# Self-attention block, 16 images, 8 heads: scores of a head made once in blocks of 128 queries instead of a maximum pass over 512 queries and a second score pass

## The chip, the cores and the metric

The kernel runs on one core of one Trainium2 chip. A core has four engines that compute, each with its own instruction stream: TensorE (matmuls, called PE in the profile; its weight loads are PEld), VectorE (DVE), ScalarE (ACT) and GpSimd (POOL). SyncE (SP) issues the DMA transfers. Engines meet only at semaphores. TensorE writes to PSUM, eight banks of 512 f32 columns on 128 partitions; VectorE and ScalarE read it, GpSimd cannot. The metric is the device time of the program in microseconds (us); lower is better.

## The reference

```python
B, N, heads, d = 16, 32 * 32, 8, 64            # 512 channels
qkv  = x @ w_qkv + b_qkv                        # [B, N, 8, 192]
q, k, v = split(qkv, 3)
attn = softmax(einsum('bxhd,byhd->bxyh', q, k) * d ** -0.5, over y)
res  = einsum('bxyh,byhd->bxhd', attn, v)
out  = res @ w_out + b_out + x
```

Input, weights and output are f32.

## The kernel before

**Precision.** Every operand is split into a high f16 part and a low f16 part (the rest), and a product is made of three f16 matmuls, hi x hi, hi x lo and lo x hi, summed in f32 in PSUM.

**Staging.** For each of the 16 images the kernel projects q and k of one head for 512 tokens at a time (12 matmuls of 512 columns, `fill`, L577), v for 128 tokens and four heads at a time (12 of 256 columns), runs attention per head, transposes the result (`transpose`, L586) and projects it (12 of 512 columns). Splitting is done by ScalarE (high parts) and VectorE (low parts).

**Attention.** Scores are kept transposed, keys on partitions and queries on columns, so that the exponentials are at once the stationary operand of the value product. The softmax then needs its maximum as a term of the product: rows of `k_shift` hold the constant 4096 and rows of `q_shift` hold minus the maximum over 4096, so the second matmul of each score tile (L634) adds both the low part of q and the shift. A unit is 512 queries of one head; its work is:
- first pass (`row_max_tile`, L596): q stationary, 512 keys on columns, 8 matmuls; VectorE reduces each to a maximum per query (L852). The results are joined (L856), transposed (L604) and written as shift rows (L862).
- second pass (`step_scores`, L632 and L634): for each of 8 key tiles two matmuls of 512 columns.
- two exponentials of each tile (`exp_tile`): f32 (`p_full`, L747) and f16 (`p_hi`, L748). Their difference is `p_lo`, made by GpSimd in six of eight steps (L493) and by VectorE in two (L871). A step is two key tiles, 1024 columns.
- values (`step_pv`, L657 to L662): per key tile and 128 queries hi x v_hi with a column of ones that gives the sum, hi x v_lo, lo x v_hi, mostly 65 columns wide. The division (L884 to L893) follows each unit.

**Order.** Tables of slots (a slot is a step) say at which slot each projection, transpose, maximum or split is issued; each engine walks the same slots and does its share, and a semaphore count per kind of work joins them. PSUM: score tiles rotate over three banks, so a tile's first matmul waits for the exponential three tiles back (L630); maxima and shift rows share two banks, fills two, and values one. In a slot TensorE issues maxima, one score tile of the next step, fills, the other score tile, late maxima, and the values of the step before:

```python
L630  wait(pe, exp_done, KEYS_PER_STEP * g + n + 1 - len(SCORE_BANKS))
```

## Time and profile before

| | |
|---|---|
| median of 3 runs | 3604.11 us (3601.85 to 3605.69) |
| profiled execution | 3603.24 us |
| its span | 3600.7 us |
| busy: TensorE, ScalarE, VectorE, GpSimd | 98%, 84%, 75%, 54% |
| mean granted TensorE clock | 0.999 of full speed |
| DMA | 144.70 MB, mean 40 GB/s |

The span reaches from the first to the last instruction in the trace. Busy time counts an instruction from its start to its end. Matmuls overlap: one is issued before the one ahead of it has ended, so what a matmul costs TensorE is the gap from its start to the next start, and that is read from the timeline. The chain that ended last is followed back from the last instruction to what released it or to the instruction before it on its engine.

### The profile page before, as it was taken

What the parts mean: (1) busy time and instruction counts of PE and PEld (TensorE: products, weight loads), DVE (VectorE), ACT (ScalarE), POOL (GpSimd) and SP (SyncE); (2) the same over time, 40 slices, a digit from 0 to 9 for tenths busy, and PEclk for the clock granted to TensorE, in tenths of its full rate; (3) what the DMA queues carried; (4) which work ended last, traced back from release to release, by engine and by line L of the source; (5) the groups of instructions that cost most, each with busy time, mean ns of one, the idle gap of its engine ahead of it and who ended that gap; (6) DMA issues with size and microseconds to landing.
All of it is one profiled execution on the core that took longest, in us unless ns stands there. A gap on an engine that the chain in (4) does not pass through costs nothing.

```text
span 3600.7 us, 93452 instructions
## 1 busy us (share of the span) xinstructions
PE 3527.6 (98%) x37132; PEld 2155.3 (60%) x37132; DVE 2689.1 (75%) x4643; ACT 3015.9 (84%) x5142; POOL 1949.6 (54%) x1022
## 2 busy tenths in 40 slices
PE   7999999999999999999999999999999999999998
PEld 4656566665666656666665666656666566665664
DVE  6777777777777777777777777777777777777775
ACT  6888878888788887888878788787888878888786
POOL 2564654556455564565645556455565555656545
PEclk9999999999999999999999999999999999999999
DMA  2011110111102011020110101112011110111101
GB/s 91 12 47 40 47 43 16 54 34 50 42 15 62 28 50 42 14 68 21 49 42 26 60 18 48 43 30 60 16 47 42 43 46 18 47 43 37 45 16 54
DMA packets 100709, 144.70 MB, mean 40 GB/s; under 512 B 16192, under 2 KB 48960, under 8 KB 100288
## 3 DMA queue, kind: packets, MB, share of 16 engines
q1 hardware_dynamic: 100288, 138.74, 13.0%
q8 instruction: 307, 5.03, 0.6%
q14 instruction: 114, 0.93, 0.1%
HBM read 71.57 MB, written 33.55 MB: 29 GB/s over the span
## 4 chain that ended last, share of the span: by engine, by line
PE 84%; ACT 5%; POOL 4%; issue 3%; DVE 2%; DMA 0%; SPq 0%; ACTq 0%; DVEq 0%
PE psum L577 33%; PE psum L596 11%; PE psum L632 10%; PE psum L634 10%; PE psum L659 4%; PE psum L657 4%; PE psum L658 4%; POOL p_lo L493 3%; PE psum L662 3%; ACT p_full L747 2%; ACT p_hi L748 2%; PE psum L586 2%; PE psum L661 1%; POOL xT_lo L487 1%; PE psum L604 1%
## 5 line engine op out<-in xcount | busy, mean ns | idle before, releaser
L493 POOL TENSOR_TENSOR p_lo<-p_full,p_hi 128x1024 f16<-128x1024 f32 x768 | 1635.5, 2130 | 1511.7 <-ACT p_hi L748 1511.7
L852 DVE TENSOR_REDUCE max_parts<-psum 128x1 f32<-128x512 f32 x2048 | 1369.1, 683 | 427.0 <-PE psum L596 425.7
L747 ACT ACTIVATE p_full<-psum,prob_bias 128x512 f32<-128x512 f32 x2048 | 1430.5, 698 | 176.8 <-PE psum L634 152.3
L748 ACT ACTIVATE p_hi<-psum,prob_bias 128x512 f16<-128x512 f32 x2048 | 1431.5, 699 | 0.0
L632 PE MATMUL psum<-q_hi_hi,k_lo_hi 128*128 128x512 f16 x2048 | 777.1, 379 | 18.2 <-ACT p_hi L748 10.3
L634 PE MATMUL psum<-q_shift,k_shift 128*128 128x512 f16 x2048 | 776.2, 379 | 0.0
L657 PE MATMUL psum<-v_parts,p_hi 128*128 128x65 f16 x6144 | 754.3, 192 | 12.0 <-POOL p_lo L493 12.0
L596 PE MATMUL psum<-k_lo_hi,q_hi_hi 128*128 128x512 f16 x2048 | 743.9, 380 | 16.8 <-DMA q_hi_hi<-q_hi_hi 4.7
L658 PE MATMUL psum<-v_parts,p_hi 128*128 128x64 f16 x6144 | 755.1, 193 | 0.0
L659 PE MATMUL psum<-v_parts,p_lo 128*128 128x65 f16 x6144 | 753.0, 194 | 0.0
L657 PEld LDWEIGHTS psum<-v_parts,p_hi 128*128 128x128 f16 x6144 | 585.8, 98 | 136.1 <-issue 22.8
L658 PEld LDWEIGHTS psum<-v_parts,p_hi 128*128 128x128 f16 x6144 | 573.3, 97 | 112.4
L659 PEld LDWEIGHTS psum<-v_parts,p_lo 128*128 128x128 f16 x6144 | 574.9, 97 | 0.0
L662 PE MATMUL psum<-v_parts,p_hi 128*128 128x129 f16 x2048 | 448.1, 219 | 0.0
L862 DVE SCALAR_TENSOR_TENSOR q_shift<-psum,identity 4x512 f16<-4x512 f32 x256 | 173.7, 679 | 315.2 <-PE psum L604 311.2
L577 PE MATMUL psum<-xT_hi,wqkv_hi 128*128 128x512 f16 x1024 | 388.8, 380 | 15.0 <-DVE xT_lo L805 15.0
L661 PE MATMUL psum<-v_parts,p_lo 128*128 128x65 f16 x2048 | 393.7, 192 | 0.0
L577 PE MATMUL psum<-xT_lo,wqkv_hi 128*128 128x512 f16 x1024 | 388.6, 380 | 0.0
L577 PE MATMUL psum<-xT_hi,wqkv_lo 128*128 128x512 f16 x1024 | 388.6, 380 | 0.0
L871 DVE TENSOR_TENSOR p_lo<-p_full,p_hi 128x1024 f16<-128x1024 f32 x256 | 318.2, 1243 | 37.5 <-ACT p_hi L748 33.5
L634 PEld LDWEIGHTS psum<-q_shift,k_shift 128*128 128x128 f16 x2048 | 200.3, 98 | 199.8
L596 PEld LDWEIGHTS psum<-k_lo_hi,q_hi_hi 128*128 128x128 f16 x2048 | 198.2, 97 | 186.3 <-DVE max_parts L852 76.5
(72 smaller groups left out, 4894.7 us busy)
## 6 DMA issues: line engine op xcount, KB each, us to landing
y_tile<-in_x SPq DMA_DIRECT2D x125, 256.0 KB, 2.8
result<-y_tile SPq DMA_DIRECT2D x125, 256.0 KB, 2.0
x_in<-in_xT SPq DMA_DIRECT2D x121, 256.0 KB, 2.9
q_hi_hi<-q_hi_hi SPq DMA_DIRECT2D x256, 64.0 KB, 1.9
k_shift<-k_lo_hi SPq DMA_DIRECT2D x256, 64.0 KB, 1.9
o_heads<-in_L_conv_w_qkv SPq DMA_DIRECT2D x12, 256.0 KB, 4.7
p_full<-in_xT SPq DMA_DIRECT2D x4, 256.0 KB, 5.2
o_heads<-in_L_conv_w_out SPq DMA_DIRECT2D x4, 256.0 KB, 3.0
```

What stands on the lines that cost most here:

```text
L493: nc.gpsimd.tensor_tensor(p_lo[:, g % LO_SLOTS, :, :], p_full[:, g % 2, :, :], p_hi[:, g % HI_SLOTS, :, :], ALU.subtract).then_inc(p_lo_re ...
L577: matmul = nc.tensor.matmul(bank(b, w)[:, 0:width], stationary, moving, start=n == 0, stop=n == TERMS - 1)
L596: nc.tensor.matmul(bank(b, w), q_hi_hi[:, h % 2, q0:q0 + P], k_lo_hi[:, h % 2, k_half * HALF:(k_half + 1) * HALF], start=True, stop=True). ...
L632: nc.tensor.matmul(scores(g, n), k_lo_hi[:, h % 2, keys], q_hi_hi[:, h % 2, cols], start=True, stop=False)
L634: nc.tensor.matmul(scores(g, n), k_shift[:, h % 2, keys], q_shift[:, h % 2, cols], start=False, stop=True).then_inc(scores_ready, 1)
L657: nc.tensor.matmul(pv[:, qt, :], hi, v_hi, start=kt == 0 and qt == 1, stop=False, skip_group_check=True)
L658: nc.tensor.matmul(pv[:, qt, 0:DIM], hi, v_lo, start=False, stop=False, skip_group_check=True)
L659: nc.tensor.matmul(pv[:, qt, :], lo, v_hi, start=False, stop=end, skip_group_check=True)
L662: last = nc.tensor.matmul(pv_first, hi, v_all, start=False, stop=end, skip_group_check=True)
L747: nc.scalar.activation(p_full[:, g % 2, n, :], scores(g, n), ACT.Exp, scale=SCALE / (W_SCALE * W_SCALE), bias=prob_bias[:, :])
L748: nc.scalar.activation(p_hi[:, g % HI_SLOTS, n, :], scores(g, n), ACT.Exp, scale=SCALE / (W_SCALE * W_SCALE), bias=prob_bias[:, :]).then_i ...
L852: nc.vector.reduce_max(max_parts[:, u % 2, q_tile, k_half:k_half + 1], bank(b, w), AX.X).then_inc(done["row_max"], 1)
```

## The change

The unit of work on scores is now a block: 128 queries of one head against all 1024 keys, 1024 columns over two PSUM banks. There are 1024 blocks, 64 per image.
- `raw_scores(n)`: 8 matmuls of 128 columns, keys stationary, leave the first product open in PSUM (no stop). It takes the place of both the first pass and L632.
- `max_over_tiles`: VectorE reduces these over the eight key tiles to 128x128 (a strided read); `turn_max`: TensorE transposes it; `shift_of_queries`: VectorE reduces it to minus the maximum per query and writes a scaled diagonal into `q_shift` by two small products.
- `shifted_scores(n)`: 8 matmuls of 128 columns add low parts and shift onto the same PSUM columns. As the shift is a diagonal now, all 64 rows of `k_shift` hold 4096.
- `exponentials(n)`: two of 128x1024, f32 and f16, one signal `p_hi_ready` at the end. GpSimd makes every `p_lo`.
- `values(n)`: 24 matmuls of 64 or 65 columns, two blocks later.
- PSUM: four banks hold two blocks of scores, three serve fills, one holds values and, in its last 128 columns, the turned maxima.
- Fills are cut into pieces of three matmuls in two phases of each slot (a slot is a block now); v is projected for all eight heads at once (512 columns) during the image before, and `xT` and `v_parts` are held twice. `oT` has eight slots instead of three.

```diff
-SCORE_BANKS, PV_BANK, RING_BANKS, FILL_BANKS = (0, 1, 2), 6, (4, 5), (3, 7)
+X_SLOTS, Y_SLOTS, S_SLOTS, PROB_SLOTS = 3, 3, 2, 3
+S_BANKS, PV_BANK, FILL_BANKS = 2, 6, (4, 5, 7)
...
+    def over_two_slots(slot, b, w):
+        plan.extend([(slot, 0, b, w, 0, 3), (slot, 1, b, w, 3, 6), (slot + 1, 0, b, w, 6, 9), (slot + 1, 1, b, w, 9, TERMS)])
...
-                nc.tensor.matmul(bank(b, w), q_hi_hi[:, h % 2, q0:q0 + P],
-                                 k_lo_hi[:, h % 2, k_half * HALF:(k_half + 1) * HALF],
-                                 start=True, stop=True).then_inc(ready["row_max"], 1)
...
+            def raw_scores(n):
+                b, h, t, queries = operands(n)
...
+                wait(pe, p_hi_ready, n + 1 - S_SLOTS)
+                for kt in range(TOKEN_TILES):
+                    keys = slice(kt * P, (kt + 1) * P)
+                    last = nc.tensor.matmul(scores(n)[:, keys], k_lo_hi[:, h % 2, keys], q_hi_hi[:, h % 2, queries],
+                                            start=kt % Q_TILES == 0, stop=False, skip_group_check=True)
+                last.then_inc(raw_scores_ready, 1)
+
+            def turn_max(n):
+                pe.wait_ge(max_map_ready, n + 1)
+                wait(pe, neg_max_ready, n)
+                wait(pe, o_ready, (n - PV_LAG) // UNIT)
+                nc.tensor.transpose(max_turned, max_map[:, n % 2, :], identity[:, :]).then_inc(max_turned_ready, 1)
+
+            def shifted_scores(n):
...
+                pe.wait_ge(shift_ready, n + 1)
+                for kt in range(TOKEN_TILES):
+                    keys = slice(kt * P, (kt + 1) * P)
+                    last = nc.tensor.matmul(scores(n)[:, keys], k_shift[:, h % 2, keys], q_shift[:, h % 2, queries],
+                                            start=False, stop=True, skip_group_check=True)
+                last.then_inc(scores_ready, 1)
...
+            for g in SLOTS:
+                if is_block(g):
+                    turn_max(g)
+                if is_block(g + 1):
+                    raw_scores(g + 1)
+                fills(g, 0)
+                if is_block(g):
+                    shifted_scores(g)
+                if is_block(g - PV_LAG):
+                    values(g - PV_LAG)
+                fills(g, 1)
...
+            def exponentials(n):
+                wait(act, p_lo_ready, n - 1)
+                act.wait_ge(scores_ready, n + 1)
+                nc.scalar.activation(p_full[:, n % 2, :], scores(n), ACT.Exp, scale=SCALE / (W_SCALE * W_SCALE),
+                                     bias=prob_bias[:, :])
+                wait(act, pv_done, n + 1 - PROB_SLOTS)
+                nc.scalar.activation(p_hi[:, n % PROB_SLOTS, :], scores(n), ACT.Exp, scale=SCALE / (W_SCALE * W_SCALE),
+                                     bias=prob_bias[:, :]).then_inc(p_hi_ready, 1)
...
+            def max_over_tiles(n):
+                dve.wait_ge(raw_scores_ready, n + 1)
+                nc.vector.tensor_reduce(max_map[:, n % 2, :], scores(n).rearrange("p (t q) -> p q t", q=P), AX.X,
+                                        ALU.max).then_inc(max_map_ready, 1)
+
+            def shift_of_queries(n):
+                h, t = head_of(n), n % HEAD_BLOCKS
+                dve.wait_ge(max_turned_ready, n + 1)
+                nc.vector.tensor_reduce(neg_max[:, n % 2, :], max_turned, AX.X, ALU.max, negate=True).then_inc(neg_max_ready, 1)
+                dve.wait_ge(neg_max_ready, n + 1)
+                for half in range(2):
+                    rows = slice(half * DIM, (half + 1) * DIM)
+                    begin = t * P + half * DIM
+                    last = nc.vector.tensor_scalar(q_shift[0:DIM, h % 2, begin:begin + DIM], identity[rows, rows],
+                                                   neg_max[rows, n % 2, :], 1 / SHIFT_UNIT, ALU.mult, ALU.mult)
+                last.then_inc(shift_ready, 1)
```

TensorE's queue of before, in the middle of the program: a first-pass tile (L596), a score tile (L632, L634), half of a projection of q and k (L577), the next score tile, a first-pass tile, the first values.

```order
L596 MATMUL psum<-k_lo_hi,q_hi_hi 128x512 [waits q_hi_hi_ready1,k_lo_done,row_max_done]
L632 MATMUL psum<-q_hi_hi,k_lo_hi 128x512 [waits exp_done]
L634 MATMUL psum<-q_shift,k_shift 128x512
L577 MATMUL psum<-xT_hi,wqkv_hi 128x512 [waits x_lo_done,qk_done]
L577 MATMUL psum<-xT_lo,wqkv_hi 128x512
L577 MATMUL psum<-xT_hi,wqkv_lo 128x512
L577 MATMUL psum<-xT_hi,wqkv_hi 128x512
L577 MATMUL psum<-xT_lo,wqkv_hi 128x512
L577 MATMUL psum<-xT_hi,wqkv_lo 128x512
L632 MATMUL psum<-q_hi_hi,k_lo_hi 128x512 [waits exp_done]
L634 MATMUL psum<-q_shift,k_shift 128x512
L596 MATMUL psum<-k_lo_hi,q_hi_hi 128x512 [waits q_hi_hi_ready1,k_lo_done,row_max_done]
```

TensorE's queue of the changed kernel at such a place, one slot g up to the first value matmul: the turned maxima of block g (L540), raw scores of g+1 (L532), three fill matmuls (L499), the shift product of g (L550), values of g-2 (L569).

```order
L540 MATMUL psum<-identity,max_map 128x128 [waits o_ready,neg_max_ready,max_map_ready]
L532 MATMUL psum<-q_hi_hi,k_lo_hi 128x128 [waits p_hi_ready]
L532 MATMUL psum<-q_hi_hi,k_lo_hi 128x128 x7
L499 MATMUL psum<-xT_hi,wqkv_hi 128x512
L499 MATMUL psum<-xT_lo,wqkv_hi 128x512
L499 MATMUL psum<-xT_hi,wqkv_lo 128x512
L550 MATMUL psum<-q_shift,k_shift 128x128 [waits shift_ready]
L550 MATMUL psum<-q_shift,k_shift 128x128 x7
L569 MATMUL psum<-v_parts,p_hi 128x65 [waits o_ready,neg_max_ready,p_lo_ready,p_hi_ready]
```

The two matmuls of a score tile stood side by side; now the second stands behind the first one of the next block and behind three fill matmuls.

ScalarE's queue of the changed kernel: f32 and f16 exponentials of a block (L645, L648), with a copy of x (L595) and the split of q (L628) and k (L634) between blocks.

```order
L645 ACTIVATE p_full<-psum,prob_bias 128x1024 [waits scores_ready,p_lo_ready]
L648 ACTIVATE p_hi<-psum,prob_bias 128x1024 [waits pv_done]
L595 CAST xT_hi<-x_in 128x512 [waits x_loaded2,qk_ready]
L628 ACTIVATE q_hi_hi<-psum,qk_bias_scaled 64x512 [waits scores_ready,qk_ready]
L645 ACTIVATE p_full<-psum,prob_bias 128x1024 [waits scores_ready,p_lo_ready]
L648 ACTIVATE p_hi<-psum,prob_bias 128x1024 [waits pv_done]
L634 ACTIVATE k_lo_hi<-psum,qk_bias_scaled 64x512
```

Each block has one pair of exponentials of 1024 columns, where the same columns took two pairs of 512.

## Rows read from the trace of the kernel before

**Rows 1.** The page: busy time by engine, the granted clock in 40 slices, the chain's shares

```profile
PE 3527.6 (98%) x37132; PEld 2155.3 (60%) x37132; DVE 2689.1 (75%) x4643; ACT 3015.9 (84%) x5142; POOL 1949.6 (54%) x1022
...
PEclk9999999999999999999999999999999999999999
...
PE 84%; ACT 5%; POOL 4%; issue 3%; DVE 2%; DMA 0%; SPq 0%; ACTq 0%; DVEq 0%
```

**Rows 2.** Waits: who waited for whom, us in total, times, longest

```profile
PEld psum L632 <- ACT p_hi L748: 30.5, 49, 1.1
...
PE psum L632 <- ACT p_hi L748: 10.3, 32, 0.8
```

**Rows 3.** Timeline 1048 to 1050 us: start, duration, engine, line, operation

```profile
1048.04 0.38 PE L634 MATMUL psum<-q_shift,k_shift 128*128 128x512 f16 x1
...
1048.54 0.69 ACT L747 ACTIVATE p_full<-psum,prob_bias 128x512 f32<-128x512 f32 x1 [0.59 <-PE psum L634]
...
1048.90 0.19 PE L657 MATMUL psum<-v_parts,p_hi 128*128 128x65 f16 x1
...
1049.12 0.68 ACT L748 ACTIVATE p_hi<-psum,prob_bias 128x512 f16<-128x512 f32 x1
...
1049.20 0.22 PE L662 MATMUL psum<-v_parts,p_hi 128*128 128x129 f16 x1
...
1049.27 0.19 PE L657 MATMUL psum<-v_parts,p_hi 128*128 128x65 f16 x1
```

**Rows 4.** Timeline of the last 36 us

```profile
3565.40 1.04 PE L586 MATMUL psum<-identity,o_heads 128*128 128x128 f32 x8
...
3595.07 0.38 PE L577 MATMUL psum<-wout_hi,oT_lo 128*128 128x512 f16 x1
...
3597.01 0.38 PE L577 MATMUL psum<-wout_hi,oT_lo 128*128 128x512 f16 x1
```

**Rows 5.** Timeline of the first 50 us, around two waits of TensorE

```profile
19.14 0.38 PE L577 MATMUL psum<-xT_hi,wqkv_hi 128*128 128x512 f16 x1 [1.44 <-DVE xT_lo L805]
...
29.56 0.38 PE L596 MATMUL psum<-k_lo_hi,q_hi_hi 128*128 128x512 f16 x1 [4.71 <-DMA q_hi_hi<-q_hi_hi]
29.78 0.27 PE L577 MATMUL psum<-wqkv_hi,xT_hi 128*128 128x256 f16 x1
29.89 0.27 PE L577 MATMUL psum<-wqkv_lo,xT_hi 128*128 128x256 f16 x1
29.98 0.69 DVE L852 TENSOR_REDUCE max_parts<-psum 128x1 f32<-128x512 f32 x1 [1.53 <-PE psum L596]
...
30.10 0.42 PE L577 MATMUL psum<-wqkv_hi,xT_hi 128*128 128x256 f16 x1
```

**Rows 6.** Groups by line and shape: count, busy us, mean ns, idle before

```profile
L493 POOL TENSOR_TENSOR p_lo<-p_full,p_hi 128x1024 f16<-128x1024 f32 x768 | 1635.5, 2130 | 1511.7 <-ACT p_hi L748 1511.7
L748 ACT ACTIVATE p_hi<-psum,prob_bias 128x512 f16<-128x512 f32 x2048 | 1431.5, 699 | 0.0
...
L852 DVE TENSOR_REDUCE max_parts<-psum 128x1 f32<-128x512 f32 x2048 | 1369.1, 683 | 427.0 <-PE psum L596 425.7
...
L825 DVE TENSOR_TENSOR v_parts<-psum,v_parts 128x256 f16<-128x256 f32 x256 | 105.4, 412 | 0.9 <-ACT v_parts L739 0.4
...
L739 ACT CAST v_parts<-psum 128x256 f16<-128x256 f32 x256 | 96.8, 378 | 123.6 <-PE psum L577 119.1
...
L721 ACT CAST oT_hi<-psum 128x512 f16<-128x512 f32 x128 | 74.8, 585 | 170.1 <-PE psum L586 170.1
...
L893 DVE SCALAR_TENSOR_TENSOR o_heads<-psum,inv_sum,o_heads 128x64 f32<-128x64 f32 x256 | 72.8, 284 | 9.1
```

**Rows 7.** Timeline 1307 to 1309.5 us: an exponential's end and the matmul waiting for it

```profile
1308.08 0.68 ACT L748 ACTIVATE p_hi<-psum,prob_bias 128x512 f16<-128x512 f32 x1
...
1308.82 0.39 PE L632 MATMUL psum<-q_hi_hi,k_lo_hi 128*128 128x512 f16 x1
```

**Rows 8.** Windows: first to last score matmul; busy us of PE, PEld, DVE, ACT, POOL

```profile
46.60:3568.10 3521.50, 3477.87 (x36822) 2128.16 (x36820) 2646.59 (x4571) 2987.29 (x5089) 1944.25 (x1013) 1.00 0.13 38
```

749 lines of the change are left out of this document (308 added, 441 removed).

## The prediction

> **What bounds the kernel now.** I read the shares of busy time first. TensorE is busy 98% of the span, at full clock in all forty slices, ScalarE 84%, VectorE 75%, GpSimd 54% [rows 1]. The chain that ended last runs 84% through TensorE and only 5% through ScalarE [rows 1]. The table of waits says the same from the other side: TensorE's waits for the exponentials, of its weight loads and of its matmuls, are 30.5 and 10.3 us in 3600 [rows 2]. So the time of today is the sum of TensorE's issue gaps. In the timeline ten gaps of the 65-column value matmuls, each with new weights, lie between 1048.90 and 1049.20, 0.03 us each, and the 129-column one takes 0.06 to 0.07 (0.056 by its columns) [rows 3]; nine gaps of 512 columns lie between 3595.07 and 3597.01, 0.216 each, and eight f32 transposes take 1.04 in all, 0.13 each at most and 0.11 taken, since the last one's tail is in it [rows 4]; 256 columns take 0.11 [rows 5]. The durations in the rows, 0.38 for 512 columns, overlap each other and are not these prices.
>
> What keeps TensorE from waiting is the order. Three single score banks rotate, and a score tile waits for an exponential three tiles back; row maxima, fills and values stand in the queue between. That must be read before the change is priced.
>
> **TensorE's work after the change.** Removed: 2048 first-pass matmuls of 512 columns, 2048 x 0.216 = 442 us. Scores: 4096 of 512 columns (885 us) become 16384 of 128 columns, at 0.056 us 918 us, +33. The price of 128 columns is bounded from below by its columns, 0.216 / 4 = 0.054, and from above by the f32 transposes of 128 columns, 0.13 [rows 4]; the nearest row is the 129-column matmul, between 0.056 and 0.07 [rows 3], and I take 0.056, since the gap of 512 columns leaves 2 ns beyond the columns' own time. (At 0.13 the ring below would grow by 15 x 0.074 = 1.1 us and the time by 1140; no f16 matmul of the trace is near that.) Values: 24576 x 0.03 = 737 against 20480 x 0.03 + 2048 x 0.056 = 729, +8. Transposes of maxima: 1024 instead of 256 at 0.11, +85. The value projection, now 512 columns wide for 15 of the 16 batches, -6. Sum -442 + 33 + 8 + 85 - 6 = -322 us. Were TensorE still the bound, the span would be near 3280.
>
> **The wait that takes its place.** Two slots of two banks hold a block's scores from the first product until the second exponential has read them. The order rows show what TensorE does in block slot g: transpose the maxima of g; raw scores of g+1, whose first matmul waits for p_hi_ready, that is for both exponentials of block g-1 (same slot of banks); three fill matmuls; the shift product of g; values of g-2; three fill matmuls. TensorE runs in order, so the shift product of g is queued behind the raw scores of g+1, and ScalarE's exponentials of g wait for that shift product. This closes a ring with a period of one block: exponentials of g-1, raw g+1, three fills, shift g, exponentials of g. Nothing in it overlaps anything else in it. Behind the waiting raw matmul stand the fills, the shift product and so ScalarE itself, which is idle exactly while TensorE does the work.
>
> The ring, piece by piece:
> - Last shift matmul's issue to the first exponential's start. Before, L634 was issued at 1048.04 and the exponential that waited began at 1048.54 [rows 3]: 0.50, of which 0.216 are its columns; with 0.056 instead, 0.34.
> - The two exponentials of 128x1024, a shape that the trace lacks. At 512 columns the second starts 0.58 after the first (1048.54, 1049.12) [rows 3] and one lasts 699 ns; ScalarE's copies from PSUM take 378 ns at 256 columns and 585 at 512 [rows 6], 207 per 256 and so 0.41 us for 512 more. Start to start 0.99, the last one 1.11, together 2.10. No pair of rows gives a lower slope, so I take 2.10 as the low end; the high end is both terms doubled, 1.16 + 1.40 = 2.56. I take the low end because a duration has a fixed part that doesn't double.
> - End of the exponential to the waiting matmul: 1308.08 + 0.68 = 1308.76 to the matmul's 1308.82 [rows 7], 0.06.
> - Raw scores: 8 x 0.056 = 0.45. Fills: 3 x 0.216 = 0.65. Shift product up to its last issue: 7 x 0.056 = 0.39.
>
> Sum 0.34 + 2.10 + 0.06 + 0.45 + 0.65 + 0.39 = 3.99 us a block, where before a block's worth took 3521.5 / 1024 = 3.44 [rows 8].
>
> The Trainium skill ("ScalarE: Activation LUTs", What ACT_TABLE_LOAD costs) gives an ACTIVATE with a pointer bias as 280 ns + 0.833 ns a column, neighbours overlapping by 93 ns. At 512 columns that is 707 where the trace has 699 [rows 6], so they agree within 8 ns. At 1024 its pair is an estimated 2.17 instead of 2.10, which would put the sum 70 us higher.
>
> **What stays hidden, and why.** Take the last issue of shift g as zero; the exponentials of g end at 0.34 + 2.10 = 2.44, and raw g+2 could start at 2.50.
> - TensorE's own rest of the slot: values 24 x 0.03 = 0.72, fills 0.65, transpose 0.11, together 1.48. It waits some 1.0 us in each block. Fifty-six slots have three fill matmuls more (2.13, still hidden); six in the first batch have a whole value projection more (about 2.8, over by 0.3 each, 2 us).
> - Maximum of g+1 on VectorE: raw g+1 was issued by -1.04; a reduce starts about 0.2 after its columns (29.56 to 29.98, less 0.216 [rows 5]). VectorE takes 683 ns at 512 columns and 412 at 256 [rows 6], so some 1.22 at 1024: done near 0.4. Its reads are strided over eight key tiles, of which the trace has no case; doubled it is 2.45 and done near 1.65.
> - Shift of g+1: transpose issued at 1.48, its reduce starts at about 1.7; 128 columns on the line of the two rows are 0.28; two small products are at most 0.28 each (the 128x64 row) [rows 6]; ready by about 2.7 with the handovers. Needed at 2.50 + 0.45 + 0.65 = 3.60. So 0.9 us is to spare; VectorE's other work in a slot (q, k, v, output splits of 0.4 to 0.76 each, at most two, plus the division of a unit every fourth) uses it without the deadline being missed.
> - GpSimd now makes every low part: 1024 x 2.13 = 2181 us [rows 6], plus its other work, 1949.6 - 1635.5 = 314 [rows 1, 6], 2500 of some 4100. The exponentials of g need the low part of g-2 only, values of g-2 come two periods later. Hidden; moving 256 low parts off VectorE is worth nothing on this path.
> - ScalarE's copies and splits (at most three of 0.58 to 0.70 in a slot) lie in its own 1.9 us of waiting. Its exponentials shrink from 2 x 1431 us to an estimated 2048 x 0.99 = 2030, but they are in series with TensorE now.
> - SP issues the same q and k copies, x, y and result transfers; heads are projected a head ahead, so none is on the ring. The larger x and value buffers cost nothing here.
>
> **The sum.** 1024 x 3.99 = 4086. In 64 of the 1024 slots phase 0 has no fill matmuls (no value work in the last batch, no projection of outputs at head 0 and in batch 0): -64 x 0.65 = -42. Ahead of the first block 46.6 us as now, where the first scores start [rows 8]. After the last exponential: low part 2.2, values 0.7, seven projections of 12 x 0.216 = 18.1 with five groups of four transposes of 0.44, and 3.7 from the last matmul to the end (3597.01 to 3600.7) [rows 4]: 27. Span 4086 - 42 + 47 + 27 = 4118; the profiled run took 2.5 us beyond its span (3603.24 - 3600.7), which gives 4121. The median of the runs is 0.9 above the profiled one. With the few overruns above I say 4125.
>
> **Rivals.**
> - The maximum or VectorE's queue joins the ring. For it: the strided read has no row. At 2.45 us the reduce ends at 1.65, then in the fuller slots 1.5 us of other work, then 0.28 + 0.56: 4.0 against the 3.60 needed. Perhaps a quarter of the blocks lose 0.4, +100, 4225. Against: the VectorE rows from PSUM lie on one line of about 1.06 ns a column [rows 6].
> - The 128x1024 exponential costs twice the 128x512 one, for instance because it crosses two banks: +0.46 a block, 4125 + 471 = 4596. Against: the slope of the two copies [rows 6].
> - TensorE's clock. The granted clock is full throughout the steady part, but there TensorE never rests. In the prologue it waited 4.71 us before L596 at 29.56, and at 30.10 a 256-column matmul lasts 0.42 instead of 0.27 us, the 1.2 GHz level; after a wait of 1.44 us (19.14) the 512-column one lasts its usual 0.38 [rows 5]. The new rests are 1.0 us each, nearer the second case, but come 1024 times. At the low level TensorE's 3.03 us of work per block doubles to 6.1 and binds: some 6250.
> - Not slower: the ring doesn't bind and TensorE does, 3280. This needs the exponentials of g to be over when TensorE reaches raw g+2, 1.48 us after the last shift issue, so the pair must end within 1.1 us of its start. Already at 512 columns the trace's pair needs 0.58 + 0.70 = 1.28. The break-even with today needs a ring of 3.45, a pair of 1.56: 0.54 below the lowest slope.
>
> The Trainium skill ("Perfetto Trace Analysis", Optimizing Scalar/DVE Operations) says that where ScalarE is not saturated but causes bubbles elsewhere, splitting its instructions may let work end sooner. The change goes the other way, one signal a block instead of four; by that rule the bubbles are to be expected, and no row of before shows them since TensorE hardly waits there.
>
> **Chances.** Ring as summed 0.86; VectorE in the ring 0.06; exponential near its high end 0.04; clock 0.02; not slower 0.02. The small terms of the ring (two handovers, sixteen short issue gaps, the slope) are each known to a few hundredths; minus 0.07 and plus 0.17 a block give 4050 and 4300, which takes in the first rival and leaves the others out. A measurement of this kernel tells 0.2% from no change; every case but the last is far beyond. Faster 0.02, same 0.01, slower 0.97.
>
> **What would show it.** Right: TensorE busy under 85%, its longest wait the raw-score weight load on the second exponential, about 1 us times 1024; ScalarE waiting for the shift product, 1.5 to 1.9 us less what it copies meanwhile; the chain of waits alternating between both engines; exponentials of 1.11 us. The first step is wrong if the raw scores don't wait; the sizes are wrong if an exponential is over 1.2 us, eight short matmuls take over 0.5, or shift products wait for VectorE's q_shift. A low granted clock would be the third rival.

## The result, and the profile after

The changed kernel takes 4832.42 us (median of 4 runs, 4824.06 to 4839.39) against 3603.74 (4 runs, 3601.85 to 3605.69): ratio 1.3408 [1.338, 1.3437]. The sign and the place were forecast; the size was not. 4125 was predicted, 4300 was the upper end, and 707 us are missing. The page of the kernel after, with the lines that answer to those of before [rows 1], the chain's shares by engine and then by line:

```profile
PE 3568.0 (74%) x48748; PEld 2449.9 (51%) x48748; DVE 3649.4 (75%) x5545; ACT 2696.0 (56%) x2974; POOL 2476.9 (51%) x1278
...
PEclk9999999999999999999999999999999999999998
...
PE 38%; DVE 31%; ACT 19%; issue 11%; POOL 2%; ACTq 0%; SPq 0%; DMA 0%; POOLq 0%; DVEq 0%
DVE q_shift L752 20%; ACT p_hi L648 12%; PE psum L499 11%; PE psum L550 10%; ACT p_full L645 7%; PE psum L532 7%; DVE neg_max L747 3%; DVE max_map L741 2%; PE psum L571 2%; PE psum L569 2%; PE psum L570 2%; PE psum L540 2%; DVE o_heads L764 2%; POOL p_lo L419 1%; PE psum L508 1%
```

TensorE is down from 98% to 74% busy, as forecast, and its waits for the exponentials have come. But the costliest line of the chain is one that the prediction priced at "at most 0.28" and called hidden: L752, VectorE's two small products that turn the negated maxima into the diagonal operand of the shift. The table of waits (waiter <- releaser: us in total, times, longest), to be set beside [rows 2]:

```profile
ACT p_full L645 <- PE psum L550: 2084.8, 1022, 5.0
PEld psum L550 <- DVE q_shift L752: 742.7, 451, 3.8
PEld psum L532 <- ACT p_hi L648: 648.3, 722, 1.8
PE psum L532 <- ACT p_hi L648: 620.4, 875, 1.5
```

L532 are the raw scores and L550 the shift product. The first and the last two lines are the predicted ring. The second isn't in it: in 451 blocks of 1024 the shift product stood still because VectorE had not made its operand, which the prediction had named among the signs of being wrong. The groups by line and shape (count, busy us, mean ns), beside [rows 6]:

```profile
L419 POOL TENSOR_TENSOR p_lo<-p_full,p_hi 128x1024 f16<-128x1024 f32 x1024 | 2185.1, 2134 | 2303.2 <-ACT p_hi L648 2303.2
L752 DVE TENSOR_SCALAR q_shift<-identity,neg_max 64x64 f16<-64x64 f32 x2048 | 1332.0, 650 | 50.8
L741 DVE TENSOR_REDUCE max_map<-psum 128x128 f32<-128x1024 f32 x1024 | 1248.4, 1219 | 324.5 <-PE psum L532 324.5
L645 ACT ACTIVATE p_full<-psum,prob_bias 128x1024 f32<-128x1024 f32 x1024 | 1142.0, 1115 | 2087.8 <-PE psum L550 2084.8 <-POOL p_lo L419 3.0
L648 ACT ACTIVATE p_hi<-psum,prob_bias 128x1024 f16<-128x1024 f32 x1024 | 1133.4, 1107 | 0.0
```

Four of the five sizes are the predicted ones: 1.115 and 1.107 us for the exponentials (1.11), 1.219 for the strided maximum (1.22), 2.134 for the low part (2.13). The fifth, 64 columns in a mean of 650 ns, is not. The same line by its shortest, median and longest (ns), with the first and last start:

```profile
L752 DVE TENSOR_SCALAR q_shift<-identity,neg_max x2048: 245/252/2202, 41.6 to 4799.8; 64x64 f16<-64x64 f32 x187
```

Half of the products take 252 ns or less, and the longest 2202. The 2202 is close to the time of the GpSimd instruction, and that is where to look.

### The profile page after: what moved, and what is told of

Same layout as the page of the kernel before. It is cut to its first block, busy times and chain, and to the rows that moved or that the text cites. A ratio compares the mean times of both kernels' runs of the same rounds, so it can differ in the third digit from the quotient of the medians.

```text
span 4836.9 us, 115141 instructions
## 1 busy us (share of the span) xinstructions
PE 3568.0 (74%) x48748; PEld 2449.9 (51%) x48748; DVE 3649.4 (75%) x5545; ACT 2696.0 (56%) x2974; POOL 2476.9 (51%) x1278
## 4 chain that ended last, share of the span: by engine, by line
PE 38%; DVE 31%; ACT 19%; issue 11%; POOL 2%; ACTq 0%; SPq 0%; DMA 0%; POOLq 0%; DVEq 0%
DVE q_shift L752 20%; ACT p_hi L648 12%; PE psum L499 11%; PE psum L550 10%; ACT p_full L645 7%; PE psum L532 7%; DVE neg_max L747 3%; DVE max_map L741 2%; PE psum L571 2%; PE psum L569 2%; PE psum L570 2%; PE psum L540 2%; DVE o_heads L764 2%; POOL p_lo L419 1%; PE psum L508 1%
## 5 line engine op out<-in xcount | busy, mean ns | idle before, releaser
L419 POOL TENSOR_TENSOR p_lo<-p_full,p_hi 128x1024 f16<-128x1024 f32 x1024 | 2185.1, 2134 | 2303.2 <-ACT p_hi L648 2303.2
L645 ACT ACTIVATE p_full<-psum,prob_bias 128x1024 f32<-128x1024 f32 x1024 | 1142.0, 1115 | 2087.8 <-PE psum L550 2084.8
L741 DVE TENSOR_REDUCE max_map<-psum 128x128 f32<-128x1024 f32 x1024 | 1248.4, 1219 | 324.5 <-PE psum L532 324.5
L752 DVE TENSOR_SCALAR q_shift<-identity,neg_max 64x64 f16<-64x64 f32 x2048 | 1332.0, 650 | 50.8
L648 ACT ACTIVATE p_hi<-psum,prob_bias 128x1024 f16<-128x1024 f32 x1024 | 1133.4, 1107 | 0.0
L532 PE MATMUL psum<-q_hi_hi,k_lo_hi 128*128 128x128 f16 x8192 | 643.5, 222 | 629.2 <-ACT p_hi L648 620.4
L550 PE MATMUL psum<-q_shift,k_shift 128*128 128x128 f16 x8192 | 648.9, 224 | 567.0 <-DVE q_shift L752 566.9
L550 PEld LDWEIGHTS psum<-q_shift,k_shift 128*128 128x128 f16 x8192 | 518.6, 100 | 914.4 <-DVE q_shift L752 742.7
L532 PEld LDWEIGHTS psum<-q_hi_hi,k_lo_hi 128*128 128x128 f16 x8192 | 477.7, 99 | 923.4 <-ACT p_hi L648 648.3
L569 PE MATMUL psum<-v_parts,p_hi 128*128 128x65 f16 x8192 | 887.8, 196 | 0.0
L569 PEld LDWEIGHTS psum<-v_parts,p_hi 128*128 128x128 f16 x8192 | 779.4, 100 | 0.1
L570 PEld LDWEIGHTS psum<-v_parts,p_hi 128*128 128x128 f16 x8192 | 775.3, 99 | 0.2
L499 PE MATMUL psum<-xT_hi,wqkv_hi 128*128 128x512 f16 x1024 | 390.8, 382 | 12.9 <-DVE xT_lo L696 12.9
L499 PE MATMUL psum<-xT_lo,wqkv_hi 128*128 128x512 f16 x1024 | 390.2, 381 | 0.0
L499 PE MATMUL psum<-xT_hi,wqkv_lo 128*128 128x512 f16 x1024 | 389.9, 381 | 0.0
L540 PE MATMUL psum<-identity,max_map 128*128 128x128 f32 x1024 | 292.4, 286 | 49.7 <-DVE o_heads L764 47.1
L540 PEld LDWEIGHTS psum<-identity,max_map 128*128 128x128 f32 x1024 | 146.7, 143 | 246.2 <-issue 148.2
```

The lines of the kernel that those rows point to most:

```text
L419: nc.gpsimd.tensor_tensor(p_lo[:, n % PROB_SLOTS, :], p_full[:, n % 2, :], p_hi[:, n % PROB_SLOTS, :], ALU.subtract).then_inc(p_lo_ready, 1)
L499: matmul = nc.tensor.matmul(bank(b, w)[:, 0:width], stationary, moving, start=n == 0, stop=n == TERMS - 1)
L532: last = nc.tensor.matmul(scores(n)[:, keys], k_lo_hi[:, h % 2, keys], q_hi_hi[:, h % 2, queries], start=kt % Q_TILES == 0, stop=False, sk ...
L540: nc.tensor.transpose(max_turned, max_map[:, n % 2, :], identity[:, :]).then_inc(max_turned_ready, 1)
L550: last = nc.tensor.matmul(scores(n)[:, keys], k_shift[:, h % 2, keys], q_shift[:, h % 2, queries], start=False, stop=True, skip_group_chec ...
L569: nc.tensor.matmul(pv[:, qt, :], hi, v_hi, start=kt == 0 and qt == 0, stop=False, skip_group_check=True)
```

## One block as predicted, one that is not

The timeline of an undisturbed block (start, duration in us, engine, line, operation; xN groups N instructions):

```profile
2399.62 1.11 ACT L645 ACTIVATE p_full<-psum,prob_bias 128x1024 f32<-128x1024 f32 x1 [1.23 <-PE psum L550]
...
2400.63 1.11 ACT L648 ACTIVATE p_hi<-psum,prob_bias 128x1024 f16<-128x1024 f32 x1
...
2401.05 0.29 DVE L747 TENSOR_REDUCE neg_max<-psum 128x1 f32<-128x128 f32 x1 [0.57 <-PE psum L540]
2401.37 0.51 DVE L752 TENSOR_SCALAR q_shift<-identity,neg_max 64x64 f16<-64x64 f32 x2
...
2401.79 0.62 PE L532 MATMUL psum<-q_hi_hi,k_lo_hi 128*128 128x128 f16 x8 [0.78 <-ACT p_hi L648]
2401.82 2.13 POOL L419 TENSOR_TENSOR p_lo<-p_full,p_hi 128x1024 f16<-128x1024 f32 x1 [1.94 <-ACT p_hi L648]
...
2402.25 0.38 PE L499 MATMUL psum<-wout_hi,oT_hi 128*128 128x512 f16 x1
...
2402.90 0.50 PE L550 MATMUL psum<-q_shift,k_shift 128*128 128x128 f16 x6
...
2403.61 1.11 ACT L645 ACTIVATE p_full<-psum,prob_bias 128x1024 f32<-128x1024 f32 x1 [1.30 <-PE psum L550]
```

The period is 2403.61 - 2399.62 = 3.99 us, the forecast to the hundredth, and so are its pieces: 1.01 + 1.11 for the pair (2.10 predicted), 0.05 to the raw scores, 0.46 of raw scores, 0.65 of fills, 0.71 from the shift product's first issue to the exponential (0.39 + 0.34 = 0.73). Two of these are 0.01 to 0.02 over and two as much under, so the hundredth is partly luck. The two products end at 2401.88, having both started before GpSimd's 2401.82. Now a block 27 us later, in which output transposes stand ahead of the maxima's transpose in TensorE's queue:

```profile
2426.21 1.11 ACT L645 ACTIVATE p_full<-psum,prob_bias 128x1024 f32<-128x1024 f32 x1 [2.11 <-PE psum L550]
...
2428.11 0.29 DVE L747 TENSOR_REDUCE neg_max<-psum 128x1 f32<-128x128 f32 x1 [0.89 <-PE psum L540]
...
2428.38 0.62 PE L532 MATMUL psum<-q_hi_hi,k_lo_hi 128*128 128x128 f16 x8 [0.32 <-ACT p_hi L648]
2428.41 2.12 POOL L419 TENSOR_TENSOR p_lo<-p_full,p_hi 128x1024 f16<-128x1024 f32 x1 [1.98 <-ACT p_hi L648]
2428.43 2.41 DVE L752 TENSOR_SCALAR q_shift<-identity,neg_max 64x64 f16<-64x64 f32 x2
...
2430.90 0.62 PE L550 MATMUL psum<-q_shift,k_shift 128*128 128x128 f16 x8 [1.25 <-DVE q_shift L752]
...
2431.61 1.11 ACT L645 ACTIVATE p_full<-psum,prob_bias 128x1024 f32<-128x1024 f32 x1 [2.81 <-PE psum L550]
```

The products start at 2428.43, 0.02 us after GpSimd, and the two take 2.41 us instead of 0.51. In the chain of waits the first takes 2.14 us, as long as GpSimd's 2.12, and the second 0.26. TensorE waits 1.25 us and the block takes 5.40 (2426.21 to 2431.61). Over the whole kernel, of the 1023 distances from one block's first exponential to the next one's, 513 are 3.98 to 4.1 us, 416 are 5.1 to 5.5 (157 of them 5.41, 134 of them 5.18) and 65 are longer, up to 6.8; the mean is 4.65. In most blocks with 5.18 the transpose of the maxima had waited for a unit's division (L764), every fourth block. Call a block hit when its two products together take over 0.9 us: there are 481, with a mean period of 5.40, and the 542 others have a mean of 3.99.

The starts and ends say it for every product, not for two blocks alone: 519 of the 2048 take over 300 ns, and each of the 519 ends 0.04 to 0.05 us after an instruction of GpSimd's ends (480 times the low part L419, 39 times its other work).

The mechanism read from this: a product that begins while GpSimd's low part runs doesn't proceed until GpSimd is done, both being from SBUF to SBUF. The Trainium skill states it ("SBUF — State Buffer", Who interferes with whom): VectorE and GpSimd share a pair of ports under an exclusive lock, which the instruction that starts first keeps to its end; VectorE's tensor_scalar in a two-port mode needs it, and so do instructions with two inputs in SBUF against a GpSimd instruction that reads SBUF; "Issue order, not op shape, decides who blocks." The two blocks agree, down to a start that missed by 0.02 us. In which mode L752 runs no row shows. If it holds, "Engines meet only at semaphores", said of the chip at the start, is too narrow: no semaphore makes L752 wait for L419. It is a theory until the lock's length, its order and the operand's place are each changed alone.

## The experiments

The theory to test (the lock) says: 3.99 is the ring's own period, and the rest, some 700 us, is the products' wait. Its rival: VectorE is simply late, through its queue, whatever GpSimd does. Where runs were repeated the ratio to the kernel before has its 95% interval. Beside these runs the kernel before took 3603.03 to 3603.99 (medians).

**1. A shorter GpSimd instruction.**

```diff
-                nc.gpsimd.tensor_tensor(p_lo[:, n % PROB_SLOTS, :], p_full[:, n % 2, :], p_hi[:, n % PROB_SLOTS, :],
+                nc.gpsimd.tensor_tensor(p_lo[:, n % PROB_SLOTS, 0:P], p_full[:, n % 2, 0:P], p_hi[:, n % PROB_SLOTS, 0:P],
                                         ALU.subtract).then_inc(p_lo_ready, 1)
...
+            nc.vector.memset(p_lo[:, :, :], 0.0)
```

> The changed kernel, but GpSimd makes the low part of 128 of a block's 1024 columns; the other columns of p_lo are zero. Everything else, VectorE's small products too, stays. Theory A (a small product of q_shift waits while GpSimd's low part runs, since both are SBUF to SBUF and share a way to SBUF): the products fall from a mean of 650 ns to some 250 to 300, nearly all blocks take the ring's 3.99 us, the time is 4080 to 4160 us. Theory B (the products are slow or late by themselves, or TensorE's late transposes cost the time): products stay near 650 ns and the time near 4830. Theory C (TensorE's clock, 0.972, is the cause): the time stays above 4650.

One run: 4208.27 us, 48 above the range of theory A and far below the others. The instruction falls from 2134 to 434 ns and the products from a mean of 650 to 282, without a change to them. 340 products still take over 300 ns, 298 of them behind the short low part and 42 behind GpSimd's other instructions of 1.16 and 1.27 us, which stayed as they were:

```profile
L753 DVE TENSOR_SCALAR q_shift<-identity,neg_max 64x64 f16<-64x64 f32 x2048 | 578.4, 282 | 50.8
```

**2. The same work in four instructions of 256 columns.**

```diff
+LOW_PARTS = 4
...
+                for k in range(LOW_PARTS):
+                    cols = slice(k * TOKENS // LOW_PARTS, (k + 1) * TOKENS // LOW_PARTS)
+                    last = nc.gpsimd.tensor_tensor(p_lo[:, n % PROB_SLOTS, cols], p_full[:, n % 2, cols], p_hi[:, n % PROB_SLOTS, cols],
+                                                   ALU.subtract)
+                last.then_inc(p_lo_ready, 1)
```

> The changed kernel, but GpSimd makes each low part in four instructions of 256 columns instead of one of 1024. Theory A, if a waiting product gets through as soon as the running GpSimd instruction ends: a product waits at most some 0.6 us instead of 2.1, blocks that took 5.2 to 5.4 us take 4.0 to 4.6, the time is 4150 to 4350 us. Theory A, if GpSimd keeps the way as long as it has work queued: 4830 or more. Theory B or C: 4830, since TensorE and VectorE do the same.

One run: 4250.24 us, within the range of theory A in its first form. GpSimd works longer in all (4 x 671 ns, 2915.6 us busy instead of 2476.9), and yet the kernel is 582 us faster. VectorE and GpSimd in this kernel's timeline, in a block like the hit one above:

```profile
2426.62 2.56 POOL L422 TENSOR_TENSOR p_lo<-p_full,p_hi 128x256 f16<-128x256 f32 x4 [0.38 <-ACT p_hi L652]
...
2426.65 1.32 DVE L756 TENSOR_SCALAR q_shift<-identity,neg_max 64x64 f16<-64x64 f32 x2
```

Again the products start just behind GpSimd (0.03 us), but wait for parts of it, not for all of the 2.56 us: the lock goes by instruction. More products are slow than before (636 over 300 ns against 519), but what they take beyond 252 ns sums up to 213 us instead of 820. So it is neither GpSimd's share of time nor its amount of data.

**3. The operand out of SBUF.** The negated maximum goes to a free column of a PSUM bank, and the product is written as scalar_tensor_tensor with that column broadcast, so that only the identity is read from SBUF. The full low part stays.

```diff
-        neg_max = sb("neg_max", [P, 2, 1], f32)
...
+        neg_max = whole_bank(PV_BANK)[:, MAX_AT - 1:MAX_AT]
...
-                    last = nc.vector.tensor_scalar(q_shift[0:DIM, h % 2, begin:begin + DIM], identity[rows, rows],
-                                                   neg_max[rows, n % 2, :], 1 / SHIFT_UNIT, ALU.mult, ALU.mult)
+                    last = nc.vector.scalar_tensor_tensor(q_shift[0:DIM, h % 2, begin:begin + DIM],
+                                                          neg_max[rows, :].broadcast_to([DIM, DIM]), 1 / SHIFT_UNIT,
+                                                          identity[rows, rows], ALU.mult, ALU.mult)
```

> The changed kernel, but the negated maximum is kept in a PSUM column, and the two small products read it from there (broadcast) and only the identity from SBUF, instead of reading the identity and a scalar from SBUF in a tensor_scalar. Same engine, same place, same size. Theory A: the products no longer wait for GpSimd, last some 200 to 250 ns each, and the kernel runs at the ring as predicted: 4100 to 4170 us. Theory B or C: 4750 or more.

4166.40 us (4165.66 to 4167.93), ratio 1.1563 [1.1546, 1.1581]. The products by mean and by shortest, median and longest, and the wait of the shift product:

```profile
L752 DVE SCALAR_TENSOR_TENSOR q_shift<-psum,identity 64x64 f16<-64x64 f32 x2048 | 453.3, 221 | 48.6
```

```profile
L752 DVE SCALAR_TENSOR_TENSOR q_shift<-psum,identity x2048: 215/222/228, 41.6 to 4130.2; 64x64 f16<-64x64 f32 x187
```

```profile
PEld psum L550 <- DVE q_shift L752: 36.6, 69, 1.9
```

No product takes over 228 ns, though GpSimd's 2.13 us are as they were and some 630 of the products begin while a GpSimd instruction runs. Of the 1023 distances between blocks 680 are 3.98 to 3.99 us, 246 are 4.06, and about one in each batch is 5.2 or more; the chain is 41% TensorE, 40% ScalarE, 2% VectorE. This is the kernel that the prediction had summed, and it lies 41 us above it. Moving the operand is worth 4832.42 - 4166.40 = 666 us.

**4. The same instruction with both inputs in SBUF**, so that form and place are told apart: scalar_tensor_tensor as in 3, the maximum in SBUF as in the changed kernel.

```diff
-                    last = nc.vector.tensor_scalar(q_shift[0:DIM, h % 2, begin:begin + DIM], identity[rows, rows],
-                                                   neg_max[rows, n % 2, :], 1 / SHIFT_UNIT, ALU.mult, ALU.mult)
+                    last = nc.vector.scalar_tensor_tensor(q_shift[0:DIM, h % 2, begin:begin + DIM],
+                                                          neg_max[rows, n % 2, :].broadcast_to([DIM, DIM]), 1 / SHIFT_UNIT,
+                                                          identity[rows, rows], ALU.mult, ALU.mult)
```

> The changed kernel with the small products as scalar_tensor_tensor, identity and negated maximum both read from SBUF (the run with the maximum in PSUM differs only in where the maximum lies). By the Trainium skill (SBUF — State Buffer, the summary of its port rules) two SBUF inputs also wait for a GpSimd instruction that reads SBUF. If that holds: products near 600 ns and some 4750 to 4850 us. If only the tensor_scalar form waits: some 220 ns and 4166 us, as with the maximum in PSUM.

One run: 4838.12 us, the time of the changed kernel.

```profile
L752 DVE SCALAR_TENSOR_TENSOR q_shift<-neg_max,identity 64x64 f16<-64x64 f32 x2048 | 1274.0, 622 | 48.5
```

The same operation and shape, 622 ns here and 221 in 3. All of the 513 products that begin while a GpSimd instruction runs are slow here (over 400 ns), none of the 630 in 3. For this operation what decides is how many of its inputs come from SBUF, which is the Trainium skill's rule for two SBUF inputs ("SBUF — State Buffer", Who interferes with whom). The tensor_scalar of the changed kernel waits in the same way; whether by its scalar in SBUF or by a two-port mode no run tells apart.

The lock being settled for these products, the ring itself was tested: is 3.99 us the in-order wait that the prediction described, and can another order be faster than before? All that follow keep the maximum in PSUM, except 7.

**5. The fills behind the shift product**, so that their 0.65 us leave the ring.

```diff
                 if is_block(g + 1):
                     raw_scores(g + 1)
-                fills(g, 0)
                 if is_block(g):
                     shifted_scores(g)
+                fills(g, 0)
```

> As the run with the maximum in PSUM, and the three fill matmuls of phase 0 stand behind the shift product instead of ahead of it. The ring loses its term of 0.65 us (3.99 to 3.34 a block). But the maxima are then transposed 2.1 us after the last shift matmul, the shift is ready at some 3.15 and the shift product's last issue at 3.6: the ring through VectorE binds, 3.6 a block, 3750 us (3650 to 3800). If only the exponentials' ring counts: 3500. If the fills were not in the ring: no change from the run before, 4130.

3992.43 us (3990.82 to 3993.90), ratio 1.1081 [1.1063, 1.11], nearly 200 us above the range. Plain blocks fall from 3.99 to 3.64, as worked out, but the mean is 3.83: VectorE still needs its 0.29 + 0.46 us behind the late transpose of the maxima, the shift product waits for it in blocks with a division (4.01) or output transposes (4.1 to 4.3), and the chain is 21% VectorE. I had priced the plain block alone.

**6. The shift product ahead of the next raw scores.** Slot g: shift g, raw g+1, values g-2, fills, transpose of the maxima of g+1, fills.

```diff
             for g in SLOTS:
                 if is_block(g):
-                    turn_max(g)
+                    shifted_scores(g)
                 if is_block(g + 1):
                     raw_scores(g + 1)
-                fills(g, 0)
-                if is_block(g):
-                    shifted_scores(g)
                 if is_block(g - PV_LAG):
                     values(g - PV_LAG)
-                fills(g, 1)
+                fills(g, 0)
...
+                fills(g, 1, True)
+                if is_block(g + 1):
+                    turn_max(g + 1)
+                fills(g, 1, False)
```

> As the run with the maximum in PSUM, with TensorE's order in a slot changed: shift product of g, raw scores of g+1, values of g-2, fills, transposes of outputs, turned maxima of g+1, fills. The shift product of g no longer stands behind raw scores that wait for the exponentials of g-1, so both exponential pairs can be back to back. If the one-block ring was the cause of the loss, what binds now is the two-block ring (end of exponentials g-1, raw 0.45, reduce from 0.25 later for 1.22, transpose, reduce 0.30, products 0.45, handovers, shift product 0.45, 0.3 to the exponentials, pair 2.12: some 6.0 to 6.2 us for two blocks) or TensorE's own 3.03 us a block: 3.05 to 3.3 us a block, 3250 to 3450 us, faster than the kernel before. If the loss lay in the 128-column matmuls or the wide exponentials themselves: over 3900.

4296.48 us (4291.94 to 4299.91), ratio 1.1922 [1.1904, 1.194]: a miss by some 850 us. VectorE and TensorE in one block show why:

```profile
2400.46 1.23 DVE L744 TENSOR_REDUCE max_map<-psum 128x128 f32<-128x1024 f32 x1 [1.16 <-PE psum L534]
...
2401.72 0.74 DVE L724 SCALAR_TENSOR_TENSOR q_shift<-psum,qk_bias_scaled,q_hi_hi 64x512 f16<-64x512 f32 x1
...
2402.39 0.28 DVE L750 TENSOR_REDUCE psum<-psum 128x1 f32<-128x128 f32 x1
...
2402.70 0.46 DVE L755 SCALAR_TENSOR_TENSOR q_shift<-psum,identity 64x64 f16<-64x64 f32 x2
...
2403.22 0.62 PE L552 MATMUL psum<-q_shift,k_shift 128*128 128x128 f16 x8 [0.50 <-DVE q_shift L755]
...
2403.67 0.61 PE L534 MATMUL psum<-q_hi_hi,k_lo_hi 128*128 128x128 f16 x8
...
2404.32 1.22 DVE L744 TENSOR_REDUCE max_map<-psum 128x128 f32<-128x1024 f32 x1 [1.16 <-PE psum L534]
```

Another ring of one block: shift product g, raw scores g+1 behind it in TensorE's queue, their maximum (1.23), a split of q that stands in VectorE's queue (0.74), transpose, reduce, products, shift product g+1. From one maximum to the next 3.86 us; the mean of all blocks is 4.13. I had taken one ring apart without going round the ones that the new order closes. The chain is 54% VectorE and 1% ScalarE.

**7. The order of 6 with the original products.**

```diff
-                    last = nc.vector.scalar_tensor_tensor(q_shift[0:DIM, h % 2, begin:begin + DIM],
-                                                          neg_max[rows, :].broadcast_to([DIM, DIM]), 1 / SHIFT_UNIT,
-                                                          identity[rows, rows], ALU.mult, ALU.mult)
+                    last = nc.vector.tensor_scalar(q_shift[0:DIM, h % 2, begin:begin + DIM], identity[rows, rows],
+                                                   neg_max[rows, n % 2, :], 1 / SHIFT_UNIT, ALU.mult, ALU.mult)
```

> The order of the run before this one with the small products as in the changed kernel (tensor_scalar, identity and scalar from SBUF). In this order they start some 2.6 us after the end of the exponentials of g-1, when the low part of g-1 (2.2 us) is over and that of g has not begun, so the wait for GpSimd is met in part of the blocks only. Theory A: products of 300 to 500 ns in the mean, 3400 to 3900 us. If the order alone decided: as the run before this one.

5908.05 us (5906.83 to 5914.61), ratio 1.64 [1.6373, 1.6427]. The expected time was far off, with that of 6. The products are the only edit against 6, and they cost 1612 us here: 1237 of the 2048 take over 300 ns (519 in the changed kernel), since they come late in each block, and they lie on the ring. Part of the 1612 goes with TensorE's clock, whose mean granted share is 0.894 here and 0.983 in 6; how much was not told apart. One hit, VectorE and GpSimd in the timeline:

```profile
2401.26 2.12 POOL L419 TENSOR_TENSOR p_lo<-p_full,p_hi 128x1024 f16<-128x1024 f32 x1 [3.28 <-ACT p_hi L651]
...
2401.82 2.72 DVE L755 TENSOR_SCALAR q_shift<-identity,neg_max 64x64 f16<-64x64 f32 x2
...
2403.34 1.15 POOL L414 TENSOR_TENSOR xT_lo<-x_in,xT_hi 128x512 f16<-128x512 f32 x1
```

The pair ends at 2404.54, when the second GpSimd instruction does (2404.49), and not 0.26 after the first: the two products, 1.60 and 1.10 us here, can each lose against another GpSimd instruction. In 226 blocks both are over 300 ns.

**8. Raw scores g+1, shift g, values g-2, fills, maxima g+1, fills.** The raw scores first, as in the changed kernel, so that their maximum has time; nothing between them and the shift product; the transpose of the maxima late in the slot before.

```diff
             for g in SLOTS:
-                if is_block(g):
-                    turn_max(g)
                 if is_block(g + 1):
                     raw_scores(g + 1)
-                fills(g, 0)
                 if is_block(g):
                     shifted_scores(g)
                 if is_block(g - PV_LAG):
                     values(g - PV_LAG)
-                fills(g, 1)
+                fills(g, 0)
...
+                fills(g, 1, True)
+                if is_block(g + 1):
+                    turn_max(g + 1)
+                fills(g, 1, False)
```

> As the run with the maximum in PSUM, with TensorE's order in a slot: raw scores of g+1, shift product of g, values of g-2, three fills, transposes of outputs, turned maxima of g+1, three fills. Against the run with the fills behind the shift product, the maxima are turned ahead of the last fills, so the shift should be ready by 2.6 to 2.9 us after the last shift matmul, where the shift product could start at 2.95: the exponentials' ring binds again, without its fills, 3.34 us a block. 1024 x 3.34 + 80 and some 20 to 60 us for blocks with a division or transposes: 3520 to 3580 us, 1 to 2% faster than the kernel before. Rival, from the run with the shift product first: VectorE's splits stand between the maximum and the shift and keep the ring through VectorE at 3.6 or more, 3750 us.

3658.07 us (3657.03 to 3659.96), ratio 1.0151 [1.0136, 1.0166]. Plain blocks take 3.33 to 3.42, the ring without its 0.65 of fills; the fuller blocks, with transposes or divisions, 3.46 to 4.7, and one a batch 5.2, which brings the mean to 3.50 and the time 78 us above the range. VectorE's splits did not hold every block at 3.6, as the rival had it.

**9. The same, with the exponentials by bank.** Four of 512 columns, and each bank of the block signalled apart in both directions.

```diff
+                    if kt % Q_TILES == 0:
+                        wait(pe, p_hi_ready if kt else first_bank_read, n + 1 - S_SLOTS)
...
+                    if kt == Q_TILES - 1:
+                        last.then_inc(first_bank_ready, 1)
...
+                for k in range(S_BANKS):
+                    cols = slice(k * HALF, (k + 1) * HALF)
+                    act.wait_ge(scores_ready if k else first_bank_ready, n + 1)
+                    nc.scalar.activation(p_full[:, n % 2, cols], scores(n)[:, cols], ACT.Exp, scale=SCALE / (W_SCALE * W_SCALE),
+                                         bias=prob_bias[:, :])
...
+                    nc.scalar.activation(p_hi[:, n % PROB_SLOTS, cols], scores(n)[:, cols], ACT.Exp, scale=SCALE / (W_SCALE * W_SCALE),
+                                         bias=prob_bias[:, :]).then_inc(p_hi_ready if k else first_bank_read, 1)
```

> As the run before this one, but exponentials, shift product and raw scores signal by bank: four exponentials of 512 columns a block, the two of the first bank as soon as its shift product is there, and raw scores of the first bank start when its two exponentials are over. Ring: four exponentials 3 x 0.58 + 0.70 = 2.43 instead of 2.12, but only one bank of raw scores (0.22) and one of shift product (0.22) in it instead of two each: 0.34 + 2.43 + 0.06 + 0.22 + 0.17 = 3.22 against 3.34. If the exponentials' ring binds: 3400 to 3480 us. If VectorE's ring or TensorE's queue binds: no gain over the run before, or a loss.

3566.73 us (3564.80 to 3567.91), ratio 0.9897 [0.988, 0.9913], so 1% faster than the kernel before, and 87 us above the range. ScalarE in a stretch of it:

```profile
2399.79 0.69 ACT L655 ACTIVATE p_full<-psum,prob_bias 128x512 f32<-128x512 f32 x1
2400.36 0.70 ACT L659 ACTIVATE p_hi<-psum,prob_bias 128x512 f16<-128x512 f32 x1
...
2402.41 0.68 ACT L659 ACTIVATE p_hi<-psum,prob_bias 128x512 f16<-128x512 f32 x1
2402.98 0.69 ACT L655 ACTIVATE p_full<-psum,prob_bias 128x512 f32<-128x512 f32 x1
```

From one block's second half (2399.79) to the next one's (2402.98) are 3.19 us, the 3.22 of the expectation. The mean over the 1023 distances, 3.41, is not. TensorE is busy 95% again; the chain is 71% TensorE and 22% VectorE. In each group of four, the block whose transpose waits for a division comes 3.58 us after the one before in the mean, the others 3.29 to 3.45. That part was not taken further.

## Why the prediction missed

- **The ring: right.** Raw scores wait for the exponentials of the block before, and the shift product and ScalarE stand behind them. 3.99 us predicted, 3.99 read in plain blocks, 3.98 to 3.99 with the lock gone; 5, 8 and 9 shorten it by taking pieces out of it. Nothing else was needed for the sign: with the products no longer waiting, 3 is still 16% slower than the kernel before.
- **The sizes that the trace of before lacked: right.** The pair of exponentials 2.12 against 2.10 (the doubled one is refuted), eight short matmuls 0.46 against 0.45, the strided maximum 1.219 against 1.22. Removing the first pass, the 442 us of the sum, gave TensorE time for which nothing waited.
- **The step that failed** is "Shift of g+1", in the part on what stays hidden: "two small products are at most 0.28 each [...]; ready by about 2.7 [...] Needed at 2.50 + 0.45 + 0.65 = 3.60. So 0.9 us is to spare". The price came from a row that reads PSUM [rows 6], and these read SBUF alone. The true deadline, by which the second of them must have begun, is the moment at which GpSimd takes up the low part, the end of the exponentials at 2.44 by the prediction's own count. With products from about 2.1 to 2.7, that count had them on both sides of it. One that begins behind it costs up to 2.2 us instead of 0.25, and the 0.9 us to spare is gone: 5.18 or 5.41 instead of 3.99 in the commonest hit blocks. What should have stopped me was in the trace of before and not among the rows read. There the shift's operand is made from PSUM, and never varies (instruction count; shortest, median and longest ns):

```profile
L862 DVE SCALAR_TENSOR_TENSOR q_shift<-psum,identity x256: 678/679/680, 45.3 to 3554.9; 4x512 f16<-4x512 f32 x128
```

  The changed kernel's doesn't read PSUM any more. And the lock itself stands in that trace, in both directions. VectorE's own low part L871, with two inputs in SBUF, usually takes 1.23 us; GpSimd's L487 usually takes 1.16:

```profile
2429.38 1.16 POOL L487 TENSOR_TENSOR xT_lo<-x_in,xT_hi 128x512 f16<-128x512 f32 x1
...
2430.08 1.54 DVE L871 TENSOR_TENSOR p_lo<-p_full,p_hi 128x1024 f16<-128x1024 f32 x1 [1.22 <-ACT p_hi L748]
...
2430.91 1.73 POOL L487 TENSOR_TENSOR xT_lo<-x_in,xT_hi 128x512 f16<-128x512 f32 x1 [0.36 <-ACT xT_hi L697]
```

  L871 begins while L487 runs and takes 1.54 us; the next L487 begins while L871 runs and takes 1.73. This happens 17 times to L871 and 32 times to GpSimd (2.26 us at the longest), too rarely to show in a mean.

  The step measures 666 us of the 707 missing (3 against the changed kernel). Of the other 41, the blocks of 4.06 and the long one of each batch, both priced as plain, make some 37 (246 x 0.07 + 16 x 1.23).
- **"GpSimd makes every low part [...] Hidden": right of what waits for GpSimd's result (3.0 us in all, in the row of L645), wrong of what waits for GpSimd's instruction.** The change put both sides of the lock into every block: a low part on GpSimd (before in three of four) and two products that read SBUF alone (before, only L871 did so in the steady part with two inputs, in the steps whose low part GpSimd did not make). Leaving every fourth low part on VectorE was not tried.
- **Rival 1** (VectorE in the ring, 4225, chance 0.06) had the engine right and the mechanism wrong: the strided read, on which it rested, costs nothing (1.219 us against 1.22 on the line of the contiguous ones). The range, made from that rival and short terms, took in no mechanism between engines. The Trainium skill's rule on the lock stood to be weighed and was not.
- **The clock: small in this kernel.** The mean granted clock is 0.972 in the changed kernel and 0.993 in 1, which has little of the lock; the 542 blocks that are not hit keep their 3.99 us in the mean.
- **A wrong count.** The prediction says "one signal a block instead of four"; before, ScalarE gave one signal for each tile of 512 columns, so two for a block's worth. No term of the sum uses it.

## What to carry over

When a small instruction gets onto a path, price it by where its operands lie and by what runs on the other engine at that moment, not by its columns: ask for each VectorE instruction with two inputs in SBUF, or a tensor_scalar from SBUF to SBUF, when GpSimd starts, and take that start as its deadline. Reading SBUF alone is not enough for the wait: the kernel before joins its maxima with a reduce from SBUF (L856), and its 256 take 160 to 163 ns, though half of them begin while GpSimd runs. One operand in PSUM, or GpSimd's instruction in pieces, took most or all of the wait away here, the first at no cost in work, the second for 0.55 us more of GpSimd's time a block. And when an order written out by hand is changed, go round every ring that in-order queues close, through each engine, and price the fullest block beside the plain one.

## What the runs showed of the hardware

- A VectorE product of 64x64 takes 252 ns (median) and up to 2202 if GpSimd's 2.13 us instruction has begun, were it 0.02 us before. It works the other way too: in the kernel before, a GpSimd instruction of 1.16 us that began 0.28 us after a VectorE one with two inputs in SBUF took 1.96. The waiting is booked as the instruction's own busy time: VectorE's 75% of the page are partly waiting, and only the distance between median and mean (252, 650) tells it. With one operand from PSUM: 215 to 228 ns in all 2048 cases.
- GpSimd's two-input instruction took 434 ns at 128 columns, 671 at 256 and 2134 at 1024, so cutting it in four costs 0.55 us per block of GpSimd's time.
- After some of TensorE's longer waits its granted clock falls for some us. In the changed kernel slow matmuls stand right behind 15 of the 35 waits of 2 us or more, and behind 10 of the 957 waits from 0.3 to 1 us. Behind one wait of 2.10 us, this is the matmul row and then the window of 2 us around it (PE, PEld, DVE, ACT and POOL busy, granted clock 0.58, between the 1.2 and 2.4 GHz levels):

```profile
2409.15 0.93 PE L550 MATMUL psum<-q_shift,k_shift 128*128 128x128 f16 x8 [2.10 <-DVE q_shift L752]
...
2410.05 0.24 PE L569 MATMUL psum<-v_parts,p_hi 128*128 128x65 f16 x1
```

```profile
2409.00:2411.00 2.00, 1.85 (x29) 1.85 (x30) 1.23 (x2) 0.83 (x1) 1.27 (x2) 0.58 0.37 114
```

  The eight matmuls take 0.93 us instead of 0.62, and the value matmul 0.24 instead of 0.19. After the ring's own wait of 0.78 us in the undisturbed block shown above they keep 0.62.
